# A four-layer norm and scan kernel: pairs of chunks in the first norm, merged strip operations, earlier narrow branches, and a second queue for the last store

## The reference

```python
x = x + attention(_gn(x), w1, b1, w2, b2, w3, b3, alpha)     # layer 0
x = x + scan_prelu(_gn(x), conv_w, conv_b, prelu_a)          # layer 1, along the last axis
x = x + attention(_gn(x), ...)                               # layer 2
x = x + scan_relu(_gn(x), W, b)                              # layer 3, along the rows

# attention: e1 = relu(w1 x + b1), e2 = relu(w2 x + b2)      64 channels each
#            y = alpha * x softmax(e1' e2)' + relu(w3 x + b3)
# scan:      s = act(W s + b) + x[t], forwards over 16 strips, then backwards over the states
```

## Time and profile before

| | us |
|---|---|
| median of 3 runs (lowest to highest) | 253.76 (253.59 to 253.97) |
| the profiled execution: its time | 253.8 |
| its span in the trace | 252.0 |
| PE busy, share of the span | 246.5, 98% |
| DVE busy | 169.1, 67% |
| ACT busy | 96.3, 38% |
| POOL busy | 87.9, 35% |
| granted TensorE clock, share of full | 1.00 |

### The profile page before, as it was taken

One profiled execution on the slowest core, in us unless ns is written; L12 is line 12 of the kernel. 1 busy time (PEld: TensorE's weight loads), 2 busy tenths in 40 slices (PEclk: granted clock), 3 DMA queues, 4 the chain that ended last, 5 costly groups with the idle time before them and its releaser, 6 DMA issues.

```text
span 252.0 us, 11079 instructions
## 1 busy us (share of the span) xinstructions
PE 246.5 (98%) x4493; PEld 219.2 (87%) x4496; DVE 169.1 (67%) x663; ACT 96.3 (38%) x231; POOL 87.9 (35%) x138
## 2 busy tenths in 40 slices
PE   7999999999999999999999999999999999999995
PEld 2778887878699999999997888878787999999995
DVE  2699656575767777777888885666757555555553
ACT  2144544535964334433445465454567000000000
POOL 0208011025357666776732400000063432333432
PEclk9999999999999999999999999999999999999999
DMA  6999100000000000000000000000000000011212
GB/s 205 403 380 419 55 0 0 4 0 0 0 4 4 0 0 0 0 0 0 0 4 0 0 0 4 0 0 0 3 1 0 3 0 0 0 42 62 83 62 83
DMA packets 5199, 11.47 MB, mean 46 GB/s; under 512 B 704, under 2 KB 3264, under 8 KB 4672
## 3 DMA queue, kind: packets, MB, share of 16 engines
q1 hardware_dynamic: 4896, 10.76, 11.5%
q10 hardware_dynamic: 288, 0.52, 0.6%
HBM read 9.19 MB, written 2.10 MB: 45 GB/s over the span
## 4 chain that ended last, share of the span: by engine, by line
PE 93%; DVE 3%; DMA 2%; issue 1%; POOL 0%; DVEq 0%; POOLq 0%
PE banks L509 46%; PE banks L395 21%; PE banks L460 11%; PE banks L407 6%; PE banks L338 2%; PE banks L426 2%; DMA x<-in_x 2%; PE banks L481 1%; PE banks L445 1%; DVE mx L818 1%; PE banks L362 1%; DVE st L708 1%; PE banks L492 0%; PE banks L373 0%; POOL rstd L1085 0%
## 5 line engine op out<-in xcount | busy, mean ns | idle before, releaser
L509 PE MATMUL banks<-state,wc 128*64 128x64 f32 x3840 | 114.9, 223 | 0.2
L509 PEld LDWEIGHTS banks<-state,wc 128*64 128x64 f32 x3840 | 114.1, 138 | 1.1 <-DVE state L908 0.4
L395 PE MATMUL banks<-xn,w 128*128 128x256 f32 x256 | 61.0, 384 | 0.0
L395 PEld LDWEIGHTS banks<-xn,w 128*128 128x128 f32 x256 | 47.1, 190 | 7.2 <-issue 1.7
L938 DVE SCALAR_TENSOR_TENSOR state<-banks,negb,inb 128x64 f32<-128x64 f32 x116 | 29.2, 282 | 24.0 <-PE banks L509 24.0
L1085 POOL TENSOR_TENSOR rstd<-gvar,mhalf 128x2 f32<-128x2 f32 (+3 forms) x13 | 15.9, 1232 | 80.3 <-DVE gvar L783 76.5
L944 DVE SCALAR_TENSOR_TENSOR sloped<-banks,par,share 128x64 f32<-128x64 f32 x120 | 30.7, 281 | 13.6 <-PE banks L509 12.5
L460 PE MATMUL banks<-probT,xT 128*128 128x256 f32 x128 | 28.9, 379 | 0.0
L460 PEld LDWEIGHTS banks<-probT,xT 128*128 128x128 f32 x128 | 24.3, 190 | 3.3
L646 ACT COPY banks<-inb 128x256 f32 (+1 forms) x28 | 10.6, 377 | 30.4 <-DVE state L954 28.0
L1138 POOL TENSOR_TENSOR share<-share,bent 128x256 f32<-128x256 f32 x29 | 17.8, 613 | 5.6 <-ACT share L647 2.5
(11 more groups left out here) (115 smaller groups left out, 231.5 us busy)
## 6 DMA issues: line engine op xcount, KB each, us to landing
w<-in_w SPq DMA_DIRECT2D x2, 1024.0 KB, 12.2
xT<-in_xT SPq DMA_DIRECT2D x4, 512.0 KB, 12.1
wc<-in_wc SPq DMA_DIRECT2D x2, 1024.0 KB, 16.6
result<-xh SPq DMA_DIRECT2D x15, 128.0 KB, 1.8
x<-in_x SPq DMA_DIRECT2D x3, 512.0 KB, 9.1
x<-in_x ACTq DMA_DIRECT2D x1, 256.0 KB, 4.5
x<-in_x SPq DMA_DIRECT2D x1, 256.0 KB, 4.3
w<-in_w ACTq DMA_DIRECT2D x1, 256.0 KB, 5.0
```

The lines of the kernel that those rows point to most:

```text
L395: mm = nc.tensor.matmul(bank[2 + m // 2][:, m % 2 * POS:(m % 2 + 1) * POS], w3[l][:, k, m * P:(m + 1) * P], xn_s[:, k], start=(k == 0), st ...
L509: mm = nc.tensor.matmul(bank[K * h + m][c:c + TILE, 0:COLS], wc[l][:, k, m * P + c:m * P + c + TILE], state[:, h, k], start=first and not ...
```

## The change

Five edits, which share semaphore counts and so go together.

1. **First image's norm by pairs.** `pair_deviations` and `pair_variances` (TensorE) and `pair_norms` (VectorE) do two chunks at a time in banks of their own. `gvar` of the first pair is signalled before that of the second. `signs` and `signed_constants` follow `normalise_first`. Seven zeros become five.
2. **Strips.** For image 3, VectorE makes state and inputs 1 and 2 of a chunk in one operation on `inb[:, 0:3]`; step 0 of each scan reads `inb[:, 0]`. GpSimd's addition to `inb[:, 0]` comes after step 0. In layer 1, identity products are in three groups, the first of them earlier. In layer 3 two steps stand ahead of the loop.
3. **Narrow branches.** They are issued for the next image: after the output products of image 0, before those of images 1 and 2. In images 2 and 3 the scores come before all products and the transposes after ten. `group_variances` of the next norm comes one product later. ScalarE normalises the next image before the exponentials, and VectorE makes `shifted` in two halves around the softmax's scaling (all of it after `gvar` in the last image).
4. **No zeros** after the transposes of the second passage.
5. **Two last queues.** SyncE stores chunks 0 to 2 of the last strip, ScalarE chunk 3.

```diff
-WARM_VARIANCES = [7, 6, 4, 7]
+WARM_VARIANCES = [5, 6, 0, 7]
...
+            def pair_deviations(p):
+                s = norm[0]
+                ks = slice(p * K // 2, (p + 1) * K // 2)
+                deviations, means = (bank[b + p][:, 0:K // 2 * SETS].rearrange("p (c s) -> p c s", s=SETS) for b in (6, 4))
+                pe.wait_ge(s.stats, (p + 1) * K // 2)
+                pe.wait_ge(s_gavg, 32)
+                nc.tensor.matmul(deviations, centre[:, 0], st[:, ks, :, 1], start=True, stop=False)
+                nc.tensor.matmul(deviations, centre[:, 1], st[:, ks, ::-1, 1], start=False, stop=True).then_inc(s.dev, 1)
+                nc.tensor.matmul(means, gavg[:], st[:, ks, :, 1], start=True, stop=True).then_inc(s.mean, 1)
+
+            def pair_variances(p):
+                s = norm[0]
+                ks = slice(p * K // 2, (p + 1) * K // 2)
+                out = bank[2 * p][:, 0:K // 2 * SETS]
+                pe.wait_ge(s.svar, p + 1)
+                nc.tensor.matmul(out, gavg[:], svar[:, ks], start=True, stop=False)
+                pe.wait_ge(s.vadd, p + 1)
+                nc.tensor.matmul(out, gavg[:], dev2[:, ks], start=False, stop=True).then_inc(s.var, 1)
...
                 def image(n, h, first=False, last=False):
+                    ready = n >= 2
+                    if first:
+                        narrow_branches(n, h)
...
+                    branch = [(m, k) for m in range(K) for k in range(K)]
+                    before_scores = 0 if ready else 5
+                    before_turns = 10 if ready else 13
+                    relu_products(0, before_scores)
                     pe.wait_ge(s.e_ready, (n + 1) * 4)
...
+                    relu_products(5, 8)
                     if first and l == 2:
                         group_variances(l, 1)
+                    relu_products(8, 9)
                     if last:
                         group_variances(l + 1, 0)
+                    relu_products(9, min(12, before_turns))
...
                     pe.wait_ge(s.pt_copied, (n + 1) * PC)
+                    if not first and not last:
+                        narrow_branches(n + 1, 1 - h)
...
+                    if first:
+                        narrow_branches(n + 1, 1 - h)
...
-                        add_inputs({2: (0, 1), 3: (2, 3)}.get(m, ()))
+                        add_inputs({1: (0, 1), 2: (2,), 3: (3,)}.get(m, ()))
...
                     turn(range(5, 8))
-                    pe.wait_ge(att[2].xT_copied, 4)
-                    keep_warm(WARM_VARIANCES[l], WARM_BANK[l])
                     return
...
-                if centred(l, r):
+                if l == 0:
+                    pair_deviations(0)
+                    pair_deviations(1)
+                    keep_warm(WARM_MEANS[l], WARM_BANK[l])
+                    pair_variances(0)
+                    pair_variances(1)
+                elif centred(l, r):
...
+                    if first:
+                        narrow_branches(n)
+                    elif not last:
+                        normalise_next()
+                    act.wait_ge(s.nmx_ready, n + 1)
...
+            act.wait_ge(scan[3].result, K)
+            act.dma_start(a["out"][:, 0, K - 1:], xh[:, 0, K - 1:]).then_inc(s_out, 16)
...
+            def pair_norms():
+                s = norm[0]
+                pairs = [slice(p * K // 2, (p + 1) * K // 2) for p in range(2)]
+                def sets(b):
+                    return bank[b][:, 0:K // 2 * SETS].rearrange("p (c s) -> p c s", s=SETS)
+                for p, ks in enumerate(pairs):
+                    image_stats(0, 0, range(p * K // 2, (p + 1) * K // 2))
+                    dve.wait_ge(s.stats, (p + 1) * K // 2)
+                    nc.vector.tensor_scalar(svar[:, ks], st[:, ks, :, 2], SETS / POS, EPS, ALU.mult, ALU.add)\
+                        .then_inc(s.svar, 1)
+                for p, ks in enumerate(pairs):
+                    dve.wait_ge(s.dev, p + 1)
+                    link(nc.vector.tensor_copy(dev[:, ks], sets(6 + p)))
+                    nc.vector.tensor_tensor(dev2[:, ks], dev[:, ks], dev[:, ks], ALU.mult).then_inc(s.vadd, 1)
+                dve.wait_ge(s.var, 1)
+                nc.vector.reduce_sum(gvar[:, pairs[0]], sets(0), AX_X).then_inc(s.gvar, 1)
...
+                dve.wait_ge(s.var, 2)
+                nc.vector.reduce_sum(gvar[:, pairs[1]], sets(2), AX_X).then_inc(s.gvar, 1)
...
                     if last:
                         set_variances(l + 1, 0)
+                    elif not first:
+                        shifted_input(range(K // 2))
...
                     if last:
                         variances(l + 1, 0)
+                        shifted_input()
+                    elif not first:
+                        shifted_input(range(K // 2, K))
...
+                for k in range(K):
+                    dve.wait_ge(norm[l].rstd, 2 + k * 2 // K)
+                    c = (N - 1) * K + k
+                    nc.vector.tensor_scalar(inb[:, 0:EARLY, k, place], xr[:, 0:EARLY, k, N - 1],
+                                            gmean[:, c:c + 1], rstd[:, c:c + 1], ALU.subtract, ALU.mult)\
+                        .then_inc(s.state[k], 1)
+                for k in range(K):
+                    dve.wait_ge(s.state[k], 1)
```

More of the change, by code:

```diff
@@ L325, in _ @@
                 sp.dma_start(a["out"][:, t], xh[:, t]).then_inc(s_out, 16)
[L326 to L329, removed]
+            sp.wait_ge(scan[3].result, K - 1)
+            sp.dma_start(a["out"][:, 0, 0:K - 1], xh[:, 0, 0:K - 1]).then_inc(s_out, 16)
             sp.wait_ge(s_out, 16 * (T - 1 + 2))
@@ L402, in attention, with narrow_branches @@
                     pe.wait_ge(s_small, 32)
-                def image(n, h, first=False, last=False):
+                def narrow_branches(n, h):
                     for k in range(K):
@@ L409, in image @@
                     mm.then_inc(s.e_mm, 1)
+                def image(n, h, first=False, last=False):
+                    ready = n >= 2
+                    if first:
+                        narrow_branches(n, h)
                     if not first:
@@ L449, in image @@
                         group_variances(l, 1)
-                    relu_branch(xn[h], 3, True, range(ahead, K))
+                    relu_products(before_turns, len(branch))
                     if l == 0:
@@ L510, in scan_step @@
                             bank[K * h + m][c:c + TILE, 0:COLS], wc[l][:, k, m * P + c:m * P + c + TILE],
-                            state[:, h, k], start=first and not seeded, stop=final and not alone,
+                            inb[:, 0, k] if zeroth else state[:, h, k],
+                            start=first and not seeded, stop=final and not alone,
                             skip_group_check=True)
                     if final and alone:
-                        add_inputs({2: (0, 1), 3: (2, 3)}.get(m, ()))
+                        add_inputs({1: (0, 1), 2: (2,), 3: (3,)}.get(m, ()))
                     elif final:
@@ L536, in relu_scan @@
                 pe.wait_ge(s_wc[3], 16)
-                with pe.Fori(0, T - 1) as i:
+                for q in range(2):
+                    scan_step(3, q, q, False)
+                with pe.Fori(0, T - 2) as i:
                     for h in range(2):
-                        scan_step(3, i * 2 + h, h, False)
+                        scan_step(3, i * 2 + 2 + h, h, False)
             def critical_norm(l, r):
@@ L583, in attention, with narrow_branches @@
                 s = att[l]
-                def image(n, h, first=False, last=False):
+                def narrow_branches(n):
                     act.wait_ge(s.e_mm, n + 1)
@@ L662, in prelu_inputs @@
                 scan_inputs(1, 1, (N - 1,), EARLY, range(1))
-                act.wait_ge(s.early, K + 1)
+                act.wait_ge(s.early, 1)
                 first_share(0, late).then_inc(s.share, 1)
@@ L813, in shifted_input @@
                                     .then_inc(s.shifted, 1)
-                    if not first:
-                        shifted_input()
                     dve.wait_ge(s.s_mm, n + 1)
@@ L973, in step @@
                 def step(q, t, h):
-                    if not (isinstance(q, int) and q == 0):
+                    if not (isinstance(q, int) and q < 2):
                         dve.wait_ge(s.taken, q)
@@ L1129, in scan_layer @@
                 bias = layer_bias(l).unsqueeze(2).to_broadcast([P, K, COLS])
-                for u in units:
-                    pool.wait_ge(s.state[u], 1)
-                pool.wait_ge(s.early, K + 1)
                 def share_bias(q, h):
@@ L1142, in scan_layer @@
                     share_bias(1, 1)
-                    pool.wait_ge(s.sloped[K - 1], 1)
-                nc.gpsimd.tensor_tensor(inb[:, 0], state[:, 0], bias, ALU.add).then_inc(s.taken, 1)
+                for u in units:
+                    pool.wait_ge(s.state[u], 2)
```

(1 more changed line is left out.)

81 lines of the change are left out of this document (38 added, 43 removed).

## The result

| | before | after |
|---|---|---|
| median (lowest to highest), us | 253.76 (253.59 to 254.44), 20 runs | 254.69 (253.69 to 257.21), 20 runs |
| ratio of after to before, 95% interval | | 1.0048 (1.0028 to 1.0068) |
| the profiled execution: time, span | 253.8, 252.0 | 256.75, 254.9 |
| its granted TensorE clock, mean | 1.00 | 0.987 |

The change makes the kernel slower by 0.5%. The forecast was 253.4, in a range of 252.7 to 254.2. More telling than the median is the spread. Before, all 20 runs lie within 0.9 us. After, they fall into three groups by their mean granted clock: ten at full clock with 253.69 to 254.42 (median 254.09), five at 0.993 with 254.97 to 255.41, and five at 0.987 with 256.75 to 257.21. The profiled execution is one of the last group.

The account below looks back on a forecast made before the run. PE was taken as the bound, busy 98% of the span, from the first narrow branch to the last scan's end. Terms 0.5 - 0.66 + 0.3 + 0.05 + 0.24 - 0.45 - 0.1 - 0.24 = -0.36 took 253.8 to 253.4, range 252.7 to 254.2.

Parts of the forecast that it names:

- The head's +0.5: First image's norm: six sums instead of three delay gvar from 8.05 to about 8.57; +0.5 us, bounds -0.2 and +0.6.
- rival C: Second passage: PE idle some 0.4 us before the first narrow branch lowers the clock; 255.2 us, chance 0.05.
- Norm by pairs: Head, first image: PE waits for gavg until 6.40, then does both pairs' sums before the first pair's variances; +0.5 us.
- five zeros end before the wait does: Head, after the variances: five products of zeros instead of seven finish within PE's wait; cost nothing.
- Rival A: Head: four-column sums are cheap or gavg comes early, so the +0.5 becomes about 0; 252.9 us, chance 0.32.
- Variances one product later: Last image, both passages: earlier scores and one more product cover PE's wait for VectorE's vadd; -0.33 us, twice.
- rival B: Last images: VectorE's copy behind four shifted operations comes late and the 0.66 is spent again; 254.1 us, chance 0.12.
- Second image: PE waits for VectorE's copy of a transpose, delayed by normalisation and shifted operations; +0.3 us second passage, +0.05 first.
- Three groups: First scan: a third group of identity products adds one more pair of changes between whole weights and tiles; +0.24 us.
- No zeros: Second passage: without zeros, PE starts some 0.1 after the first normalised chunk, at 133.24 instead of 133.71; -0.45 us.
- Second scan's start: Second scan: merged strip operations bring the third chunk's first state, bias and the following first states earlier; -0.1 us.
- Last store: End: ScalarE issues the last chunk at some 249.74 instead of SyncE at 249.98, landings otherwise as before; -0.24 us.

Follow-up runs that it names:

- a seventh: Changed kernel without the pairs, plus ten one-column memsets of a spare tile at the start of VectorE's program: 252.94 us, ratio 0.9962.
- fifteen zeros: Changed kernel with fifteen instead of thirteen products of zeros ahead of the first sums: 254.59 us, ratio 1.0031.
- zeros between: Changed kernel with two products of zeros between the first and the second pair's sums: 254.38 us, ratio 1.0027.
- gavg sooner: Changed kernel with the load of centre moved to ScalarE's queue, so that gavg is issued at 1.20, not 1.67: 253.95 us, ratio 1.0011.

## Why the prediction was wrong

**The head's +0.5 as a pure delay, and rival C's place and chance.** This is the step that failed. *Norm by pairs* priced only by how much gvar comes later, and rival C looked for a fall of the clock in the second passage's gap; there the slices show none. Against C stood "a gap of 0.71 ahead of 6.53 and the full clock in every slice", and I took it to cover the head of the changed kernel as well. It doesn't. Before, sums and one product of zeros last from 6.53 to 7.84, when the seven zeros start. After, they last from 6.44 until 8.76 even at full clock, and in half of the runs the clock falls, as the trace has it from about 8.3 on, ahead of the five zeros. Of these runs one left a trace; that the others fall in the head too rests on the experiments, six of twelve runs with the pairs alone and none of 42 in six kernels without (but one of ten in a seventh). The fall costs 1 us or 3 in such a run; at the median it is 254.69 - 254.09 = 0.6. In all, the pairs cost 1.8 where the term had 0.5: 0.6 by the fall, 0.4 by the delay, 0.3 to 0.5 in the first scan (by the traces of the kernel after and of fifteen zeros, against that without pairs), and the rest is not placed. That five zeros end before the wait does was true at full clock (8.76 + 1.24 = 10.00 against 10.12); at the lower level five end at 11.49. The Trainium skill (TensorE: Matmul & The Clock Gate, What's actually happening) has the lower rate as the default that recent activity lifts; the 0.50 behind the stretch of waits and sums agrees. I cited that rule for the wrong place and gave its rival 0.05.

**Norm by pairs.** The mechanism was right in each step: gavg binds, six sums in a row. gvar came 0.47 later (forecast 0.5) and the first chunk's normalisation 0.40; the first narrow branch, at full clock and with fifteen zeros, 0.37 (10.12 for 9.75). Rival A, *the pairs pay*, is out.

**Variances one product later.** -0.42 and -0.40 for -0.33 each, without a wait for the copy: right, and rival B did not occur.

**Second image.** 0.28 in the second passage for 0.3, with the copy as the releaser; 0.05 in the first for 0.05. Right. What ended last was `shifted`'s halves ahead of it, since moving one of them takes the whole wait away.

**Three groups.** 0.29 by the run with two, for 0.24. The Trainium skill states that a change of tiling mode drains the engine (TensorEngine Tiling (Array Packing), Key Properties); the trace agrees in that the change has a cost, 0.29 here. The whole first scan is 0.28 longer than before in the kernel without pairs, near the forecast 0.24, but 0.57 longer in the kernel after. Of the other 0.29, 0.13 is a wait of PE for the bias addition, which VectorE began 0.34 after its last input and not some 0.13 after it, and nearly 0.2 is a slower pace of the 14 forward steps. In the kernels with fifteen zeros and with zeros between, the backward half is 0.2 slower as well. No step of mine has this term. It is in all four profiled kernels that have the pairs and the other edits, not in that with the pairs alone, and in none without pairs; ten spare instructions don't bring it. Its cause stays open.

**No zeros.** -0.39 in the trace, 0.38 by the run that kept them, for -0.45. **Second scan's start:** the scan itself -0.17, gained in its first step, but norm 3 ahead of it +0.07, so -0.1 as forecast. **Last store:** -0.14 for -0.24. The second issue is on ScalarE's queue at 252.73, 0.14 after SyncE's, as forecast, but each of the two parts of 96 and 32 KB lands in 1.8, while the two of 64 KB took 1.6: that both landings would be as before was the error.

Without the pairs my terms gave -0.36 - 0.5 = -0.86, so 252.9; measured 252.87. With the pairs at full clock they give 253.4; measured 254.09. Of this 0.7, 0.33 is what the first scan lost above its term. The rest is not settled run by run. A late first rise can be part of it: in the traced execution of gavg sooner, where the rise was late, the first narrow branch comes at 10.43, 0.31 later than with fifteen zeros.

## What to carry over

Price an edit ahead of a compute engine's first real work not only by what it delays but by what it leaves the engine to do meanwhile: here waits and four-column sums in place of products of zeros went with a fallen clock in half of the runs. The kernel you start from may be close to that without showing it (0 of 80 runs, but 4 of 12 with two zeros fewer). Look at the spread and at each run's clock before you trust one profile, since half of the runs here show no fall at all, and more than half of the miss was there without one. When five edits share their counts, run them with one taken out: four of them together were a gain of 0.4%, and the fifth turned it into a loss.

## What was not expected of the hardware

- The first products run at half pace (0.43 us for 512 columns, later 0.216) while the granted clock is recorded as 1.00; the record shows later falls but not this first rise. When the rise comes differs from execution to execution: thirteen zeros took 4.32 to 5.73 us.
- After the fall the lower level held for some 7 us, although PE was busy without a gap from 9.2 on.
- 32 KB take as long to land as 96 KB, 1.8 us each, when both are issued 0.14 apart on two queues; 64 KB twice on one queue took 1.6.
